# Causal attention in three layers of a decoder: score blocks packed to three quarters, next scores ahead of the other group's transposes

## Chip, cores, metric

One core of one Trainium2 chip runs the whole program. The metric is the device time of one execution in microseconds; the times below are medians. TensorE is written PE (its weight loads PEld), VectorE DVE, ScalarE ACT, GpSimd POOL.

## What is computed

The reference is a decoder of four blocks on x of shape (8, 128, 128): eight sequences of 128 positions with 128 features. Each block is a self-attention-like layer, a cross-attention and a feed-forward layer, all with a layer norm ahead and a residual behind. The change touches the three layers with causal softmax attention, 16 heads of 8 features: the cross-attention of block 0 (L0x, with rotated queries and keys), the self-attention of block 1 (L1a) and of block 3 (L3a, rotated as well). Their core is

```python
scores = jnp.einsum('bhqd,bhkd->bhqk', Q, K) / sqrt(d)
scores = jnp.where(causal, -jnp.inf, scores)      # causal: key behind query
probs = jax.nn.softmax(scores, axis=-1)
heads = jnp.einsum('bhqk,bhkd->bhqd', probs, V)
```

Two other layers (L1x, L2x) run the same loop without a causal mask, and the change leaves theirs as it was.

## The kernel before

The eight sequences are two groups of four (`GB = 4`). Each group has its own tiles and its own four of the eight PSUM banks. Every engine runs one program for each group, and `weave` merges the two by hand-written due times: each piece of a program yields `(layer, time)` and the smallest goes next into that engine's queue. Queues are in order, so these times are the order of the work. Engines wait for each other through named steps (`s.step(name)`, `s.at(name)`).

An attention layer first makes queries and keys with features on partitions (`QT`, `KT`), values with positions on partitions and a column of ones behind each head (`vaug`, written from bank 2 by ACT in `values`, L931), and `KTm`, the keys of one sequence spread over heads (`first_keys`, L1287, on DVE; the later ones on POOL in `spread_keys`, L353). Four heads sit in a strip of 32 rows, so one matmul of a strip, with `KTm` as the moving operand, gives the scores of four heads.

Then comes `attend`: for each sequence b of each group a "turn", numbered `turn = 2*b + g`, 0 to 7 in a layer, the two groups by turns. In one turn:

- PE writes the mask into the four banks (`masked`, L441, bf16, 512 columns each) and adds the scores (`scores`, L450, four f32 matmuls of 512 columns, one for each strip and bank): heads 0 to 15, 128 queries on partitions, 128 keys each.
- DVE takes, half by half (two banks, eight heads), the maximum of each row (L1322) and subtracts it into `pr` (L1326).
- PE turns the eight 128x128 blocks of the half (`turned`, L457, transposes at L461) back into the same banks, so that keys lie on partitions. I call the halves' transposes T0 and T1.
- ACT takes the exponential into `PT` (`exponentials`, L937): one instruction of 1024 elements for the first half (L944), two of 512 for the second (L948).
- PE multiplies with the values (`weighted`, L465, eight matmuls a half into 32-column strips, here PV0 and PV1), ACT reads the result (`weighted_out`, L950, L911), and the turn's banks are free for the mask and scores of the group's next turn.

The order on PE is set in `attend` at L501 to L518: T0 at due time `beat(turn - 1, 5)`, then at `beat(turn, 0)` T1, PV0, a mask, PV1 and two masks, and at `beat(turn, 6)`, which is behind the T0 of the other group (`beat(turn, 5)`), the last mask and the next scores. So the queue reads: T0 of a turn, scores of the other group, T1, PV0, PV1 of that turn, T0 of the next turn, scores, and so on. After turn 6 the results of group 0 are turned back (`back`, L478, 16 transposes) between T0 and T1 of turn 7.

Of the kernel before, what the change touches and what calls it, by code (L numbers as in the profile page):

```python
# [14 lines left out]
P = 128  # L15
B = 8
GB = 4
# [10 lines left out]
MAGIC = 12582912.0  # L28
NEG = -1.0e30
LAYERS = ["pre", "L0a", "L0x", "L0f", "L1a", "L1x", "L1f", "L2a", "L2x", "L2f", "L3a", "L3x", "L3f"]  # L30
DESCENT = 50
# [32 lines left out]
CONSTS = [("ident", P), ("heads", HG), ("heads_x", HG), ("c0", HD), ("s0", HD), ("c3", HD), ("s3", HD), ("keepT", P), ("tri", E0 * E0), ("ident3", E2)]  # L64
BCONSTS = [("identb", P), ("causalb", P), ("alibi", H * P)]

# [26 lines left out]
def build(nc, x_d, ctx_d, mask_d, w_d, r_d, c_d, k_d, b_d, out_d, marks):  # L93
# [35 lines left out]
    class Tiles:  # L129


        def __init__(self, g):
            def own(name, shape, dt=F32):
                return sb(f"{name}{g}", shape, dt)
# [23 lines left out]
            self.vv = own("vv", [P, GB, MH, MD + 1])  # L158
            self.mx, self.rc = own("mx", [P, 2, H // 2]), own("rc", [P, H])
            self.rc3 = own("rc3", [P, GB - 1, H])  # L160
            self.co, self.coT = own("co", [P, GB, P]), own("coT", [P, W4])
# [21 lines left out]
    def pair(g, half):  # L183

        return all_banks[:, 4 * g + 2 * half:4 * g + 2 * half + 2, :]

    def heads_of(pr2):
# [27 lines left out]
    identb = bconst("identb")  # L215
    causalb = bconst("causalb")
    alibi = bconst("alibi").rearrange("p (h k) -> p h k", k=P)
# [53 lines left out]

    def keys_of(t, b):

        return t.KT[:, b * P:(b + 1) * P].unsqueeze(1).to_broadcast([P, HG, P])

    def own_head(l):

        return const("heads_x" if l == "L1x" else "heads").unsqueeze(2).to_broadcast([P, HG, P])

# [34 lines left out]
    def _(pool):  # L314
# [13 lines left out]
        def program(g):  # L328
# [7 lines left out]
            def spread_keys(n, l):  # L336

                first = 0 if l in ("L1x", "L2x") else 1
                for b in range(first, GB):
                    if g == 0 and b == 0 and l in BEHIND:  # L340
                        yield ahead(n, l, 6)
                    else:
                        yield n, ((1 + b if first == 0 else 19) if b < 2 else beat(2 * (b - 2) + g))
                    if b == first:
# [8 lines left out]
                    pool.tensor_tensor(t.KTm[:, b % 2, :, :], keys_of(t, b), own_head(l), ALU.mult).then_inc(*s.step(f"keys{b}"))  # L353
                    if b == 1:
                        yield from add_bias(n, 19, l)
# [43 lines left out]
    def _(pe):  # L399
# [7 lines left out]
        def program(g):  # L407
# [31 lines left out]
            def attend(n, l):  # L439

                def masked(b, r):  # L441

                    out = bank(r)
                    if l == "L1x":
                        mm(out, identb, alibi[:, HG * r:HG * r + HG, :], stop=False)
                    else:
                        mask = t.dmask[:, b, :] if l == "L2x" else causalb
                        mm(out, identb, mask.unsqueeze(1).to_broadcast([P, HG, P]), stop=False)

                def scores(b):  # L450
                    pe.wait_ge(*s.at(f"{l}.keys{b}"))
                    for i in range(GB):
                        r = 32 * i
                        ins = mm(bank(i), QT[r:r + 32, b * P:(b + 1) * P], t.KTm[r:r + 32, b % 2, :, :], start=False, tile_position=(r, 0))
                    ins.then_inc(*s.step(f"S{b}"))

                def turned(u):  # L457
# [41 lines left out]
                masked(0, 0)  # L499
                scores(0)  # L500
                for b in range(GB):  # L501
# [396 lines left out]
    def _(act):  # L898
# [5 lines left out]
        def program(g):  # L904
# [25 lines left out]

            def values():  # L931
                act.wait_ge(*s.at(f"{s.layer}.v"))
                V = bank(2).rearrange("p (b h d) -> p b h d", b=GB, h=H)
                act.activation(t.vaug[:, :, :, 0:HD], V, ACT.Copy).then_inc(*s.step("vaug"))

            def attend(n, l):
# [16 lines left out]

                for b in range(GB):
# [10 lines left out]
            for n, l in enumerate(LAYERS[1:STAGES + 1]):  # L965
# [57 lines left out]
                if l in ("L0x", "L3a"):  # L1023
# [10 lines left out]
                    if l == "L0x" and g == 0:  # L1034
                        read(KT, bank(1), "KTp", "KT")
                    read(QT, bank(0), "QTp", "QT")
                    if l == "L3a" or g == GROUPS - 1:
                        read(KT, bank(1), "KTp", "KT")
                    yield from attend(n, l)
                if l in ("L1a", "L1x", "L2x"):  # L1040
# [6 lines left out]
                    if l == "L1a":  # L1047
                        read(KT, bank(1), "k", "KT")
                        values()
# [107 lines left out]
    def _(dve):  # L1157
# [50 lines left out]
        def program(g):  # L1208
# [78 lines left out]
            def first_keys(l):  # L1287
                dve.wait_ge(*s.at(f"{l}.KT"))
                dve.tensor_tensor(t.KTm[:, 0, :, :], keys_of(t, 0), own_head(l), ALU.mult).then_inc(*s.step("keys0"))

            def attend(n, l):
# [8 lines left out]
                def normal_last():  # L1300
# [5 lines left out]
                                      wide(t.rc[:, :], HD), ALU.mult).then_inc(*s.step(f"co{GB - 1}"))  # L1306

                if l in ("L1a", "L3a"):
                    yield n, 19
                    first_keys(l)  # L1310
                if l in ("L1x", "L2x"):
# [4 lines left out]
                       .then_inc(*s.step("vaug"))  # L1316
                for u in range(UNITS):
                    b, half = divmod(u, 2)
# [399 lines left out]
def constants():  # L1718
# [32 lines left out]
    putb("identb", np.eye(P))  # L1751
    putb("causalb", np.where(r[None, :] > r[:, None], f(NEG), f(0.0)))
    rel = np.abs(r[None, :] - r[:, None]).astype(f)
# [85 lines left out]
```

## Time and profile before

| | us |
|---|---|
| time before, median of 3 runs (655.9 to 656.96) | 656.77 |
| the profiled execution | 654.79 |
| its span, first to last instruction | 653.0 |
| first maximum of turn 0 to the turn-back behind turn 7, layer L1a (176.93 to 220.68) | 43.75 |

The page of the profile gives for each engine the time it was busy, and the chain of work that ended last. The views by stretch and the timelines give start and length of single instructions in microseconds from the start of the span. One layer's loop of eight turns is shown by L1a; L0x (from 81.57) and L3a (from 539.77) repeat it.

### The profile page before, as it was taken

How to read it: one execution, taken by the hardware profiler on the slowest of the kernel's cores; microseconds unless marked ns; L12 is line 12 of the kernel's file. 1: busy time of each engine (PE TensorE's matmuls, PEld its weight loads, DVE VectorE, ACT ScalarE, POOL GpSimd, SP SyncE). 2: the span in 40 equal slices, each digit the busy share in tenths (PEclk: the TensorE clock that was granted, in tenths of full speed). 3: DMA queues.
4: the chain of work that ended last, by engine and by line, in shares of the span. 5: the costliest groups of instructions: out<-in, count | busy, mean ns of one | idle time of the engine just before them, and what ended most of it. 6: DMA issues, size and time to landing. Idle time of an engine off the chain costs nothing.

```text
span 653.0 us, 10939 instructions
## 1 busy us (share of the span) xinstructions
PE 553.2 (85%) x4377; PEld 364.7 (56%) x4377; DVE 467.3 (72%) x1200; ACT 262.8 (40%) x462; POOL 98.3 (15%) x101
## 2 busy tenths in 40 slices
PE   1326789978999999988997899999899978998787
PEld 0324356767455755655786765556345654675435
DVE  7688899777499779964348646996744489976685
ACT  1265645415255435525423353552321024543170
POOL 5012120004410151010002015101100022002210
PEclk9967999999799999999999999999999999999889
DMA  9900000000000000000000000000000000000001
GB/s 271 384 0 2 0 2 1 2 1 1 1 2 2 2 2 1 2 1 1 2 1 1 1 1 1 2 1 1 2 1 1 0 2 1 2 1 1 1 1 32
DMA packets 6721, 11.89 MB, mean 18 GB/s; under 512 B 528, under 2 KB 4880, under 8 KB 6416
## 3 DMA queue, kind: packets, MB, share of 16 engines
q1 hardware_dynamic: 6672, 11.21, 4.9%
q8 instruction: 34, 0.56, 0.4%
q14 instruction: 15, 0.12, 0.1%
HBM read 10.68 MB, written 0.52 MB: 17 GB/s over the span
## 4 chain that ended last, share of the span: by engine, by line
PE 62%; DVE 26%; ACT 5%; POOL 3%; issue 2%; DMA 1%; SPq 1%; DVEq 0%; ACTq 0%
PE ps L401 45%; PE ps L461 10%; DVE st L1215 3%; DVE big L1326 3%; PE ps L417 3%; DVE mx L1322 3%; PE ps L481 2%; DVE xn L1412 2%; POOL rs L334 2%; DVE x L1339 1%; DMA co<-in_ctx 1%; DVE mv L1218 1%; PE ps L608 1%; DVE ve L1220 1%; DVE s L1558 1%
## 5 line engine op out<-in xcount | busy, mean ns | idle before, releaser
L1322 DVE TENSOR_REDUCE mx<-ps 128x8 f32<-128x1024 f32 x80 | 97.4, 1218 | 13.5 <-PE ps L401 13.5
L1326 DVE TENSOR_TENSOR big<-ps,mx 128x1024 f32<-128x1024 f32 x80 | 98.0, 1225 | 6.9
L401 PE MATMUL ps<-bt 128*128 128x512 bf16 x304 | 88.2, 388 | 9.2 <-DVE ve L1220 3.9
L461 PEld LDWEIGHTS ps<-kt,big 128*128 128x128 f32 x640 | 71.1, 141 | 43.6 <-DVE big L1326 36.3
L461 PE MATMUL ps<-kt,big 128*128 128x128 f32 x640 | 85.5, 276 | 8.3 <-DVE big L1326 8.3
L334 POOL TENSOR_TENSOR rs<-ve,negh 128x4 f32<-128x4 f32 x26 | 26.4, 1015 | 371.4 <-DVE ve L1220 371.3
L401 PE MATMUL ps<-xnT,wt 128*128 128x512 f32 (+1 forms) x140 | 67.0, 606 | 5.1 <-DVE big L1604 2.6
L944 ACT ACTIVATE big<-ps 128x1024 f32<-128x1024 f32 x40 | 40.9, 1024 | 56.2 <-PE ps L461 56.2
L401 PEld LDWEIGHTS ps<-wt,big 128*128 128x128 f32 (+1 forms) x480 | 56.0, 191 | 8.5 <-issue 7.9
L401 PE MATMUL ps<-wt,big 128*128 128x128 f32 (+1 forms) x480 | 60.3, 279 | 0.0
L948 ACT ACTIVATE big<-ps 128x512 f32<-128x512 f32 x80 | 43.4, 595 | 34.5 <-PE ps L461 34.5
L353 POOL TENSOR_TENSOR KTm<-qk,kt 128x512 f32<-128x512 f32 x34 | 37.4, 1110 | 95.5 <-PE ps L401 55.8
L401 PE MATMUL ps<-big,vaug 128*32 128x128 f32 x1280 | 51.6, 279 | 0.1
L401 PEld LDWEIGHTS ps<-bt 128*128 128x128 bf16 x304 | 26.5, 99 | 42.9 <-issue 16.7
L401 PE MATMUL ps<-KTm,qk 32*128 32x512 f32 x320 | 45.6, 640 | 0.0
L911 ACT ACTIVATE xnT<-ps 128x512 f32<-128x512 f32 (+1 forms) x40 | 19.6, 490 | 61.8 <-PE ps L417 59.1
L1385 DVE SCALAR_TENSOR_TENSOR x<-ps,gw,x 128x128 f32<-128x128 f32 x80 | 22.2, 343 | 29.8 <-PE ps L401 29.0
L401 PEld LDWEIGHTS ps<-xnT,wt 128*128 128x128 f32 (+1 forms) x140 | 24.1, 189 | 29.5 <-issue 19.2
L1339 DVE TENSOR_TENSOR x<-ps,x 128x512 f32<-128x512 f32 x16 | 11.1, 691 | 39.9 <-PE ps L401 39.9
L401 PEld LDWEIGHTS ps<-big,vaug 128*32 128x32 f32 x1280 | 30.0, 109 | 16.3 <-ACT big L948 9.5
L1412 DVE TENSOR_SCALAR xn<-x,mv,rs 128x128 f32<-128x128 f32 x96 | 28.1, 356 | 9.0 <-POOL rs L334 8.3
L401 PE MATMUL ps<-wt,xnT 128*128 128x128 f32 (+2 forms) x256 | 31.2, 275 | 3.1 <-DVE big L1560 1.5
(276 smaller groups left out, 775.3 us busy)
## 6 DMA issues: line engine op xcount, KB each, us to landing
wt<-in_weights SPq DMA_DIRECT2D x1, 1664.0 KB, 15.2
wt<-in_weights SPq DMA_DIRECT2D x1, 1603.0 KB, 9.9
wt<-in_weights SPq DMA_DIRECT2D x6, 256.0 KB, 9.1
rowt<-in_rows SPq DMA_DIRECT2D x1, 975.0 KB, 5.7
wt<-in_weights SPq DMA_DIRECT2D x1, 832.0 KB, 11.5
wt<-in_weights SPq DMA_DIRECT2D x1, 608.0 KB, 16.3
wt<-in_weights SPq DMA_DIRECT2D x1, 580.0 KB, 5.5
x<-in_x SPq DMA_DIRECT2D x2, 256.0 KB, 3.1
```

What stands on the lines that cost most here:

```text
L334: pool.tensor_tensor(out, src, negh[:, :], ALU.pow).then_inc(*s.step(name + "_r"))
L353: pool.tensor_tensor(t.KTm[:, b % 2, :, :], keys_of(t, b), own_head(l), ALU.mult).then_inc(*s.step(f"keys{b}"))
L401: return pe.matmul(out, lhsT, rhs, start=start, stop=stop, **k)
L417: ins = pe.transpose(seq(bk, b), src[:, b, :], ident)
L461: ins = pe.transpose(heads_of(pair(g, u % 2))[:, i, j, :], pr[:, (u % 2) * HH + HG * i + j, :], ident)
L911: act.activation(out, src, ACT.Copy).then_inc(*s.step(name))
L944: act.activation(P2, T2, ACT.Exp, scale=SCALES[l][half]).then_inc(*s.step(f"exp{u}.1"))
L948: act.activation(P2[:, i, :, :], T2[:, i, :, :], ACT.Exp, scale=SCALES[l][half]).then_inc(*s.step(f"exp{u}.{i}"))
L1322: dve.tensor_reduce(top, S, AX.X, ALU.max).then_inc(*s.step())
L1326: dve.tensor_tensor(pr[:, half * HH:(half + 1) * HH, :].rearrange("p (i j) k -> p i j k", i=2), S, top.unsqueeze(3).to_broadcast([P, 2, HG ...
L1385: dve.scalar_tensor_tensor(x[:, b, :], bank(banks[e])[:, b * P:(b + 1) * P], gw[:, b, e:e + 1], x[:, b, :], ALU.mult, ALU.add).then_inc(*s ...
L1412: dve.tensor_scalar(xn[:, b, :], x[:, b, :], t.mv[:, b, 0:1], t.rs[:, b:b + 1], ALU.subtract, ALU.mult).then_inc(*s.step("xn"))
```

## The change

For the layers in `CAUSAL` queries 0 to 63 ("early") no longer meet keys 64 to 127, which the mask made zero anyway. Scores of four heads then fill 384 columns of a bank instead of 512, on two half strips of partitions: partitions 0 to 63 hold the first two heads of a strip, 64 to 127 the other two; each has two blocks of 128 keys for late queries and two of 64 for early ones.

- Scores become 16 f32 matmuls on tiles of 32 rows and 64 columns, eight of 256 columns and eight of 128; the mask covers 256 columns of a bank.
- The maximum is taken for a whole turn at once: 1024 elements for late and 512 for early queries; each half is subtracted in two instructions (256 and 512 elements).
- Three transposes a bank instead of four.
- Exponentials: one of 512 elements and two of 256 (on 64 partitions each) for the first half, two of 256 and two of 256 on 64 partitions for the second. The products wait for the whole half.
- For odd heads the two halves of the keys lie exchanged. So ACT writes the keys twice (`KTw`, 512 and 256 columns), and the values of even heads alone; DVE writes those of odd heads with the halves exchanged (`odd_values`, two copies of 256 elements on 64 partitions, due ahead of `first_keys` in L1a and L3a).
- POOL zeroes a part of `PT` in L0x and L3a (`blank`).
- The next scores are due at `beat(turn, 4)`, ahead of the other group's T0 at `beat(turn, 5)`.

The core of the diff:

```diff
+                def packed_scores(b):
+                    pe.wait_ge(*s.at(f"{l}.keys{b}"))
+                    for late in (1, 0):
+                        for pairs_of in range(2):
+                            for i in range(GB):
+                                r = 32 * i
...
+                                ins = mm(out, Q, K, start=False, tile_position=(r, HK * pairs_of), skip_group_check=True)
+                    ins.then_inc(*s.step(f"S{b}"))
...
+                for b in range(GB if l in CAUSAL else 0):
+                    turn, more = 2 * b + g, b + 1 < GB
+                    yield n, beat(turn - 1, 5)
+                    packed_turned(2 * b)
+                    yield n, beat(turn, 0)
+                    packed_turned(2 * b + 1)
+                    packed_weighted(2 * b)
+                    if more:
+                        masked(b + 1, 1)
+                    packed_weighted(2 * b + 1)
+                    if more:
+                        masked(b + 1, 3)
+                        pe.wait_ge(*s.at(f"{l}.OT{2 * b}"))
+                        masked(b + 1, 0)
+                        yield n, beat(turn, 4)
+                        pe.wait_ge(*s.at(f"{l}.OT{2 * b + 1}"))
+                        masked(b + 1, 2)
+                        packed_scores(b + 1)
...
+            def keys(need):
+                read(t.KTw[:, :, 0:P], four(bank(1)), need, "KTn")
+                read(t.KTw[:, :, P:P + HK], four(bank(1))[:, :, 0:HK], need, "KT")
...
+                    if half == 0:
+                        act.wait_ge(*s.at(f"{l}.T{u}.1"))
+                        act.activation(P2[:, :, :, HK:P], T2[:, :, 0:4, :], ACT.Exp, scale=scale).then_inc(*s.step())
+                    else:
+                        for i in range(2):
+                            act.wait_ge(*s.at(f"{l}.T{u}.{i}"))
+                            act.activation(P2[:, i, :, HK:P], T2[:, i, 0:4, :], ACT.Exp, scale=scale).then_inc(*s.step())
...
+                    for c in range(2):
+                        rows = slice(c * HK, (c + 1) * HK)
+                        act.activation(P2[rows, :, 2 * c:2 * c + 2, 0:HK], T2[rows, :, 4:6, :], ACT.Exp, scale=scale).then_inc(*s.step(f"exp{u}"))
...
+            def odd_values(l):
+                dve.wait_ge(*s.at(f"{l}.v"))
+                dve.wait_ge(*s.at(f"{l}.vaug_even"))
...
+                dve.tensor_copy(t.vaug[early, :, 1:H:2, 0:HD], V[late, :, 1:H:2, :]).then_inc(*s.step())
+                dve.tensor_copy(t.vaug[late, :, 1:H:2, 0:HD], V[early, :, 1:H:2, :]).then_inc(*s.step("vaug"))
...
+                        dve.tensor_reduce(of_late, late, AX.X, ALU.max).then_inc(*s.step())
+                        dve.tensor_reduce(of_early, early, AX.X, ALU.max).then_inc(*s.step())
```

## Rows read from the trace of the kernel before

**Rows 1.** The page: engines (busy us, share, instructions); shares of the chain

```profile
PE 553.2 (85%) x4377; PEld 364.7 (56%) x4377; DVE 467.3 (72%) x1200; ACT 262.8 (40%) x462; POOL 98.3 (15%) x101
...
PE 62%; DVE 26%; ACT 5%; POOL 3%; issue 2%; DMA 1%; SPq 1%; DVEq 0%; ACTq 0%
```

**Rows 2.** Busy time of one turn of L1a: us, engines (instructions), clock, DMA

```profile
187.05:192.25 5.20, 5.20 (x64) 3.13 (x60) 4.80 (x4) 2.83 (x5) 1.04 (x1) 1.00 0.00 0
```

**Rows 3.** Timeline of PE over that turn: start us, length us, instruction, count

```profile
187.05 1.09 PE L461 MATMUL ps<-kt,big 128*128 128x128 f32 x8
188.07 0.64 PE L401 MATMUL ps<-big,vaug 128*32 128x128 f32 x16
188.65 0.39 PE L401 MATMUL ps<-bt 128*128 128x512 bf16 x1
188.97 0.64 PE L401 MATMUL ps<-big,vaug 128*32 128x128 f32 x16
189.54 0.61 PE L401 MATMUL ps<-bt 128*128 128x512 bf16 x2
189.99 1.04 PE L461 MATMUL ps<-kt,big 128*128 128x128 f32 x8
190.86 0.38 PE L401 MATMUL ps<-bt 128*128 128x512 bf16 x1
191.17 1.14 PE L401 MATMUL ps<-KTm,qk 32*128 32x512 f32 x8
192.25 0.33 PE L461 MATMUL ps<-kt,big 128*128 128x128 f32 x1
```

**Rows 4.** Timeline of ACT over the same turn

```profile
187.74 1.08 ACT L948 ACTIVATE big<-ps 128x512 f32<-128x512 f32 x2 [0.85 <-PE ps L461]
...
189.68 0.38 ACT L911 ACTIVATE td<-ps 128x256 f32<-128x256 f32 x1 [0.51 <-PE ps L401]
191.12 1.02 ACT L944 ACTIVATE big<-ps 128x1024 f32<-128x1024 f32 x1 [1.06 <-PE ps L461]
```

**Rows 5.** Timeline of DVE over the same turn

```profile
188.51 1.23 DVE L1326 TENSOR_TENSOR big<-ps,mx 128x1024 f32<-128x1024 f32 x1
189.66 1.21 DVE L1322 TENSOR_REDUCE mx<-ps 128x8 f32<-128x1024 f32 x1
```

**Rows 6.** Groups by line and shape: busy us, mean ns, idle before

```profile
L1282 DVE TENSOR_TENSOR big<-ps,kt 128x256 f32<-128x256 f32 x8 | 3.0, 414 | 0.0
L1654 DVE TENSOR_REDUCE s<-ps 128x4 f32<-128x512 f32 x2 | 1.4, 686 | 2.9 <-PE ps L401 2.9
...
L1145 ACT ACTIVATE big<-ps,colt 64x512 f32<-64x512 f32 x2 | 1.4, 682 | 0.3 <-PE ps L401 0.3
```

**Rows 7.** Timeline of L1a: T0 of turns 1 and 6, end of the loop

```profile
184.80 1.04 PE L461 MATMUL ps<-kt,big 128*128 128x128 f32 x8
...
210.82 1.04 PE L461 MATMUL ps<-kt,big 128*128 128x128 f32 x8
...
220.68 0.66 PE L417 MATMUL ps<-kt,co 128*128 128x128 f32 x4
```

**Rows 8.** Timeline ahead of the first turn of L1a

```profile
174.97 0.60 ACT L934 ACTIVATE vaug<-ps 128x512 f32<-128x512 f32 x1 [0.29 <-PE ps L401]
...
175.72 1.14 PE L401 MATMUL ps<-KTm,qk 32*128 32x512 f32 x8
...
176.93 1.22 DVE L1322 TENSOR_REDUCE mx<-ps 128x8 f32<-128x1024 f32 x1 [1.53 <-PE ps L401]
```

**Rows 9.** Timeline of DVE ahead of the first turn, L0x, then L3a

```profile
78.83 0.69 DVE L1289 TENSOR_TENSOR KTm<-qk,kt 128x512 f32<-128x512 f32 x1
...
80.23 0.69 DVE L1289 TENSOR_TENSOR KTm<-qk,kt 128x512 f32<-128x512 f32 x1 [0.71 <-ACT qk L911]
...
81.57 1.23 DVE L1322 TENSOR_REDUCE mx<-ps 128x8 f32<-128x1024 f32 x1 [0.64 <-PE ps L401]
...
539.77 1.22 DVE L1322 TENSOR_REDUCE mx<-ps 128x8 f32<-128x1024 f32 x1 [0.64 <-PE ps L401]
```

More of the change, by code:

```diff
@@ L29 @@
 NEG = -1.0e30
+CAUSAL = ("L0x", "L1a", "L3a")
+HK = P // 2
+PK = 6 * HK
 LAYERS = ["pre", "L0a", "L0x", "L0f", "L1a", "L1x", "L1f", "L2a", "L2x", "L2f", "L3a", "L3x", "L3f"]
@@ L215, in build @@
     identb = bconst("identb")
[L216 removed]
+    corner = bconst("corner")
     alibi = bconst("alibi").rearrange("p (h k) -> p h k", k=P)
@@ L343, in spread_keys @@
                         yield n, ((1 + b if first == 0 else 19) if b < 2 else beat(2 * (b - 2) + g))
+                    if b == first and l in ("L0x", "L3a"):
+                        pool.wait_ge(*s.at(f"{l}.qrot"))
+                        pool.wait_ge(*s.at(f"{l}.krot"))
+                        pool.memset(t.PT[:, :, 0:HK], 0.0).then_inc(*s.step("blank"))
                     if b == first:
@@ L499, in attend @@
                 masked(0, 0)
-                scores(0)
-                for b in range(GB):
+                if l in CAUSAL:
+                    packed_scores(0)
+                else:
+                    scores(0)
+                for b in range(GB if l in CAUSAL else 0):
[16 more added lines that the diff above has]
+                        packed_scores(b + 1)
+                for b in range(0 if l in CAUSAL else GB):
                     turn, more = 2 * b + g, b + 1 < GB
@@ L952, in weighted_out, with packed_exponentials @@
                     read(t.ot[b][:, 2 * half * P:2 * (half + 1) * P], bank(2 * half)[:, 0:2 * P], f"O{u}", f"OT{u}")
-                for b in range(GB):
+                def packed_exponentials(u):
+                    half = u % 2
+                    P2 = PT[:, half * HH:(half + 1) * HH, :].rearrange("p (i j) k -> p i j k", i=2)
+                    T2 = packed(pair(g, half))
+                    scale = SCALES[l][half]
+                    if u >= 2:
+                        act.wait_ge(*s.at(f"{l}.O{u - 2}"))
+                    if half == 0:
+                        act.wait_ge(*s.at(f"{l}.T{u}.1"))
+                        act.activation(P2[:, :, :, HK:P], T2[:, :, 0:4, :], ACT.Exp, scale=scale).then_inc(*s.step())
+                    else:
+                        for i in range(2):
+                            act.wait_ge(*s.at(f"{l}.T{u}.{i}"))
+                            act.activation(P2[:, i, :, HK:P], T2[:, i, 0:4, :], ACT.Exp, scale=scale).then_inc(*s.step())
+                    if u < 2 and l in ("L0x", "L3a"):
+                        act.wait_ge(*s.at(f"{l}.blank"))
+                    for c in range(2):
+                        rows = slice(c * HK, (c + 1) * HK)
+                        act.activation(P2[rows, :, 2 * c:2 * c + 2, 0:HK], T2[rows, :, 4:6, :], ACT.Exp, scale=scale).then_inc(*s.step(f"exp{u}"))
+                for b in range(GB if l in CAUSAL else 0):
+                    turn = 2 * b + g
+                    yield n, beat(turn - 1, 5)
+                    packed_exponentials(2 * b)
+                    yield n, beat(turn, 0)
+                    packed_exponentials(2 * b + 1)
+                    weighted_out(2 * b)
+                    weighted_out(2 * b + 1)
+                for b in range(0 if l in CAUSAL else GB):
                     turn = 2 * b + g
@@ L1047, in program @@
                     if l == "L1a":
-                        read(KT, bank(1), "k", "KT")
+                        keys("k")
                         values()
@@ L1316, in attend @@
                        .then_inc(*s.step("vaug"))
-                for u in range(UNITS):
+                for u in range(UNITS if l in CAUSAL else 0):
+                    b, half = divmod(u, 2)
+                    yield n, beat(2 * b + g, 1 + half)
+                    blocks, strips = all_banks[:, GB * g:GB * (g + 1), 0:PK], slice(2 * half, 2 * half + 2)
+                    late = bass.AP(tensor=blocks.tensor, offset=blocks.offset, ap=[blocks.ap[0], blocks.ap[1], [4 * HK, 2], [1, P]])
+                    early = blocks[:, :, 2 * HK:4 * HK].rearrange("p i (c k) -> p i c k", c=2)
+                    of_late, of_early = (t.mx[:, k, :].rearrange("p (i c) -> p i c", i=GB) for k in range(2))
+                    if half == 0:
+                        dve.wait_ge(*s.at(f"{l}.S{b}"))
+                        dve.tensor_reduce(of_late, late, AX.X, ALU.max).then_inc(*s.step())
+                        dve.tensor_reduce(of_early, early, AX.X, ALU.max).then_inc(*s.step())
+                        dve.wait_ge(*s.last())
+                    if u >= 2:
+                        dve.wait_ge(*s.at(f"{l}.T{u - 2}.1"))
+                    out = pr.rearrange("p (i j) k -> p i j k", i=GB)[:, strips, :, :]
+                    dve.tensor_tensor(out[:, :, 1, :].rearrange("p i (c k) -> p i c k", c=2), early[:, strips, :, :],
+                                      of_early[:, strips, :].unsqueeze(3).to_broadcast([P, 2, 2, HK]), ALU.subtract).then_inc(*s.step())
+                    dve.tensor_tensor(out[:, :, 0:3:2, :], late[:, strips, :, :],
+                                      of_late[:, strips, :].unsqueeze(3).to_broadcast([P, 2, 2, P]), ALU.subtract).then_inc(*s.step(f"sub{u}"))
+                for u in range(0 if l in CAUSAL else UNITS):
                     b, half = divmod(u, 2)
```

61 lines of the change are left out of this document (51 added, 10 removed).

## Prediction

> **What bounds the kernel now.** Start with the page: PE is busy 85% of the span, DVE 72%, and the chain that ended last runs 62% over PE and 26% over DVE [rows 1]. An average hides the stages, so next take one turn in the middle of L1a: 5.20 us, PE busy 5.20 of them, DVE 4.80, ACT 2.83, clock 1.00 [rows 2]. Then the timeline of PE in that turn shows what the 5.20 are: T1 from 187.05, PV0 from 188.07, a mask, PV1, two masks, the other group's T0 from 189.99, a mask, the scores from 191.17, and the next T1 at 192.25 [rows 3]. No step waits: each starts when the one ahead has left the array. ACT works beside it: the long exponential (191.12 to 192.14) lies under the scores, the short pair under T1 and PV0 [rows 3, 4]. So PE's own work sets the turn, DVE has 0.4 us to spare, and ACT's time, 2.83, costs nothing as long as PE has something else to do meanwhile.
>
> **The work of a turn after the change.** PE: eight transposes follow each other at 0.109 us (189.99 to 190.86) [rows 3]; four fewer of sixteen save 0.44. Masks: two in a row take 0.45, so one of 512 columns 0.22, and half the columns save 0.11 each, 0.43 for four. PV0 and PV1 stay at 0.57 each. Scores take 1.08 now, in two passes of 512 columns at 0.43 each (a pass over 128 columns takes 0.109) and some 0.2 to load and drain [rows 3]. Afterwards each of eight tiles takes two passes of 256 and two of 128 columns, 0.65 in all; if all eight run at once the scores take 0.75 to 0.87, and I take 0.80. No row shows eight tiles at once: the nearest are four strips of columns (the products, 16 records in 0.57) and four of rows (the scores themselves). If tiles in the same rows took turns it would be 1.45. With 0.80 PE's own work falls from 5.20 to about 4.05 us a turn.
>
> DVE: 1024 elements take 1.22, a step 1.15 behind the one ahead (188.51 to 189.66) [rows 5]; 512 take 0.69 and 256 take 0.41 [rows 6]. A turn is then maxima 1.14 + 0.69 + 0.10 and twice 0.33 + 0.61 for the subtractions, 3.9 us. T0 can start 3.01 after the first maximum starts instead of 2.54, T1 0.94 behind it.
>
> ACT: 512 elements 0.60, two of them 1.08, so 0.49 apart; 256 take 0.38 [rows 4], and with the same overlap of 0.10 are 0.28 apart. An instruction on 64 partitions is no shorter: 64x512 takes 0.68 [rows 6]. The seven exponentials of a turn take 0.49 + 5 x 0.28 + 0.38 = 2.27 in a row.
>
> **Where the new order puts them.** Now the due times. Behind PV1 and the masks stand, at `beat(turn, 4)`, the wait for the last read of the results, the last mask and the next scores; only then, at `beat(turn, 5)`, T0 of the other group. Queued behind that wait are all of PE's next pieces. What PE ran beside the exponentials, the other group's scores between T0 and T1, is now ahead of T0. From T0 on nothing but T1 (0.65) and PV0 is left to cover 2.27 us of exponentials. The cover is gone, so the loop goes through ACT and back:
>
> - T0 start to first exponential: six transposes 0.65, 0.06 for the load behind the scores, and 0.26 from the end of the slot to ACT (190.86 to 191.12) [rows 3, 4]: 0.97
> - seven exponentials: 2.27; handover to PV1: 0.06 (bounds 0.05 and 0.15, the pair ending at 188.82 ahead of PV1 at 188.97 [rows 3, 4])
> - PV1 to ACT's read: 0.71 (188.97 to 189.68); the read 0.38; handover 0.06 [rows 3, 4]
> - last mask 0.21, scores 0.80, and the next T0 starts.
>
> Sum 0.97 + 2.27 + 0.06 + 0.71 + 0.38 + 0.06 + 0.21 + 0.80 = 5.46 us a turn against 5.20: PE waits about 1.4 us in each. DVE's 3.01 from the scores to T0 lies beside this and is covered; if it were not, this path alone would be scores 0.80 + 3.01, below 5.46.
>
> **One layer.** Before, L1a takes 7.87 us from the first maximum (176.93) to T0 of turn 1 (184.80), 26.02 to T0 of turn 6 (210.82), 9.86 to the end of its loop (220.68) [rows 7, 8]. After: the start is 3.01 + 0.97 + 2.27 + 0.06 to PV1, then 0.71 + 0.38 + 0.06 + 0.21 + 0.80, together 8.47, so +0.60. Five turns 5 x 5.46 = 27.30, so +1.28. The end has no further scores: 3.30 to PV1 of turn 6, 0.57, T0 of turn 7 0.65, 16 turn-backs 1.75, half of T1 and the handover 0.59, four exponentials 1.26, PV1 0.7: 8.8, so -1.06, since DVE held T0 and T1 there before. A layer's loop: +0.82; three layers: +2.5 us.
>
> **Ahead of the loop.** In L1a the values left ACT at 174.97 + 0.60, off the path; the scores started at 175.72 and DVE at 176.93 [rows 8]. Now the even heads' copy ends at 175.35, then DVE's two copies 0.74, then the keys' product 0.69 (0.08 overlapped), the scores 0.80, and handovers of 0.06: the first maximum at 177.68, +0.75. The wait for these copies stands in PE's queue ahead of masks and scores, and in DVE's ahead of the keys' product. In L0x DVE sits idle 0.71 and 0.64 between its key products and the first maximum [rows 9]; four copies of 0.33 to 0.41 and a key read that ends 0.28 later leave the first maximum at 81.91 instead of 81.57: +0.34, and the same in L3a, whose idle times are alike [rows 9]. Bounds for the three: 0.3 (all in idle time) and 2.5 (each like L1a's). POOL's zeroing and its key products have over a turn's time; I put them at nothing, and at 0.5 us if they slow DVE. ACT's second key read is in the 0.28. Sum ahead of the loops: +1.4.
>
> Total: 654.79 + 2.5 + 1.4 = 658.7 on the profiled execution, whose span is 653.0 with 1.8 us around it. It lies 2.0 below the median of the runs shown, so I add the 3.9 to 656.77: **660.7 us**.
>
> **Rivals.** First, the waits are covered after all: PE starts the other group's transposes while the last mask waits. Then a turn costs PE's own 4.05 us, and a layer 0.6 - 5 x 1.15 - 1.06 = -6.2; with +1.4 ahead the time is 639.6. For it: PE and DVE do lose a fifth of their work. Against it: every group of matmuls starts in the order of the queue, none ahead of one that stands before it [rows 3]. Chance 0.13, with all values over 0.2% faster.
>
> Second, tiles that share rows take turns, so that packing doesn't pay on PE: scores of 1.45 instead of 0.80. Six scores of a layer lie on the loop, 18 x 0.65 = +11.7: 672.4. A value between (pairs of passes overlap, 1.03) gives 664.8. Chance 0.20 for both. The products speak against it: 16 records on all 128 rows take 0.57, where 16 single passes of 0.109 would take 1.74 [rows 3], so tiles in the same rows, but other columns, do run together. The Trainium skill ("TensorE: Matmul & The Clock Gate", Part 3, The mechanism) says that weight loads overlap with running matmuls only where the row group differs. By that rule the second case holds; the products' rows disagree with it, and that is why it has no more than 0.15 of these 0.20.
>
> Third, no difference: exponentials 0.26 apart and scores 0.75 take 0.05 + 0.12 off each turn; over 18 turns that is -3.1, and copies hidden in idle time take another 1: 656.6. Chance 0.10.
>
> The forecast, ACT in the loop with all eight tiles at once, has 0.57: 658.2 to 664, the upper end with handovers of 0.15 (18 x 0.18). Within 0.2% (1.3 us) is about what a measurement can't tell from no change. So slower 0.57 + 0.20 = 0.77, within 0.10, faster 0.13. The range 656.0 to 672.5 takes in the bounds of scores and handovers and leaves out the first rival and little above.
>
> **What would show it.** In the profile after: a turn of 5.4 to 5.6 us in which PE is busy no more than 4.3 with a wait for ACT ahead of PV0, PV1 and the last mask, and the chain running over ACT in the three layers; DVE near 3.9; scores of 0.8 us, 1.45 in the second rival. A turn near 4.1 with PE full would mean the first rival. A lower clock than 1.00 in the loop, since PE idles more, or a DVE that ends last, would make me wrong in a way that no sum here has.

## The result, and the profile after

| | before | after |
|---|---|---|
| median of four executions | 656.87 us | 673.16 us |
| profiled execution | 654.79 us, span 653.0 | 673.12 us, span 671.3 |
| granted clock, mean over the span | 0.972 | 0.957 |
| PE busy | 553.2 us | 540.1 us |
| DVE busy | 467.3 us | 448.4 us |
| ACT busy | 262.8 us | 275.7 us |

The changed kernel is slower: ratio 1.0236, interval 1.0201 to 1.0271, where 660.7 (1.006) was forecast. One of the four executions took 1042.06 us and is left out of this ratio; the other three average 672.2 us, and nothing below explains the slow one.

PE and DVE have less to do, as intended, and the median went up by 16.3 us. The page of the changed kernel (engines, then shares of the chain; its answer before is [rows 1]) shows the shift from PE to ACT:

```profile
PE 540.1 (80%) x4850; PEld 367.2 (55%) x4857; DVE 448.4 (67%) x1260; ACT 275.7 (41%) x564; POOL 100.7 (15%) x105
...
PE 51%; DVE 25%; ACT 15%; issue 4%; POOL 3%; DMA 1%; SPq 1%; DVEq 0%; ACTq 0%
```

ACT's share of the chain rose from 5% to 15%, PE's fell from 62% to 51%. One undisturbed turn of L1a, timeline of PE and ACT together (start, length, instruction, count, idle time before and what ended it), to be read against [rows 3, 4]:

```profile
218.50 1.53 PE L505 MATMUL ps<-kt,big 128*128 128x128 f32 x12
...
219.47 0.60 ACT L1053 ACTIVATE big<-ps 128x512 f32<-128x512 f32 x1 [2.08 <-PE ps L505]
...
219.96 0.77 ACT L1062 ACTIVATE big<-ps 64x256 f32<-64x256 f32 x2
...
220.76 0.66 ACT L1057 ACTIVATE big<-ps 128x256 f32<-128x256 f32 x2
...
220.78 0.65 PE L425 MATMUL ps<-big,vaug 128*32 128x128 f32 x16 [0.76 <-ACT big L1062]
...
221.30 0.77 ACT L1062 ACTIVATE big<-ps 64x256 f32<-64x256 f32 x2
...
222.13 0.64 PE L425 MATMUL ps<-big,vaug 128*32 128x128 f32 x16 [0.48 <-ACT big L1062]
...
222.84 0.38 ACT L996 ACTIVATE xn<-ps 128x256 f32<-128x256 f32 x1 [0.35 <-PE ps L425]
...
223.28 0.28 PE L425 MATMUL ps<-bt 128*128 128x256 bf16 x1 [0.18 <-ACT xn L996]
...
223.49 0.91 PE L425 MATMUL ps<-KTm,qk 32*64 32x256 f32 x32
```

PE waits for ACT three times in the turn: 0.76 ahead of PV0, 0.48 ahead of PV1, 0.18 ahead of the last mask. The next T0 starts at 224.33, so the turn takes 5.83 us. Five turns of L1a from the busy-time view (stretch, length, busy us of PE, PEld, DVE, ACT, POOL, then granted clock, DMA share, GB/s), the answer to [rows 2]:

```profile
193.79:199.56 5.77, 4.41 (x89) 2.94 (x81) 3.77 (x6) 3.30 (x9) 1.04 (x1) 1.00 0.00 0
199.56:206.18 6.62, 5.20 (x89) 3.23 (x81) 3.77 (x6) 3.30 (x9) 1.04 (x1) 0.86 0.01 2
206.18:212.67 6.49, 5.17 (x88) 3.70 (x81) 3.77 (x6) 3.30 (x9) 0.00 (x0) 0.88 0.00 0
212.67:218.50 5.83, 4.41 (x89) 2.94 (x81) 3.77 (x6) 3.30 (x9) 0.00 (x0) 1.00 0.01 3
218.50:224.33 5.83, 4.41 (x89) 2.94 (x81) 3.77 (x6) 3.30 (x9) 0.00 (x0) 1.00 0.01 3
```

PE is busy 4.41 of 5.83 where it was busy 5.20 of 5.20. Two of the turns are longer by 0.79 and 0.66 because the clock was at its lower level (1.2 GHz) in part of them.

The loops run from the first maximum of a layer to the turn of its outputs. Their marks in the changed kernel, first DVE (the maxima of L1a and L3a), then PE; before they are in [rows 7 to 9]:

```profile
185.09 1.23 DVE L1455 TENSOR_REDUCE mx<-ps 128x8 f32<-128x1024 f32 x1 [0.47 <-PE ps L425]
...
555.72 1.22 DVE L1455 TENSOR_REDUCE mx<-ps 128x8 f32<-128x1024 f32 x1 [1.14 <-PE ps L425]
```

```profile
233.52 0.65 PE L441 MATMUL ps<-kt,co 128*128 128x128 f32 x4
...
603.36 0.66 PE L441 MATMUL ps<-kt,co 128*128 128x128 f32 x4
```

With the same marks in all layers the 18.3 us between the two spans divide as follows:

| stretch | before | after | more |
|---|---|---|---|
| start to L0x's first maximum | 81.57 | 82.03 | 0.46 |
| L0x's loop | 43.72 | 49.10 | 5.38 |
| to L1a's first maximum | 51.64 | 53.96 | 2.32 |
| L1a's loop | 43.75 | 48.43 | 4.68 |
| to L3a's first maximum | 319.09 | 322.20 | 3.11 |
| L3a's loop | 43.72 | 47.64 | 3.92 |
| rest | 69.5 | 68.0 | -1.5 |

14.0 of the 18.3 us lie in the three loops, for which 2.5 were forecast. The stretches ahead of L1a and L3a hold the starts of these layers. L1a's start, from PE's last projection of the inputs to the first maximum, takes 4.24 us (180.85 to 185.09) where it took 3.05 (173.88 to 176.93), so +1.19 at a clock of 1.00. L3a's start, from PE's last rotation of queries and keys, takes 4.98 (550.74 to 555.72) where it took 2.65 (537.12 to 539.77), so +2.33. Ahead of L1a's start the clock was at its lower level for some 10 us against some 7 before (0.57 over 153 to 161 us and 0.66 over 170 to 175 us; before, 0.51 over 163 to 170); the other 1.13 us of that stretch lie there.

### The profile page after: what moved, and what is told of

Read it like the earlier page. It is cut to its first block, busy times and chain, and to the rows that moved or that the text cites. A ratio compares the mean times of both kernels' runs of the same rounds, so it can differ in the third digit from the quotient of the medians.

```text
span 671.3 us, 12049 instructions
## 1 busy us (share of the span) xinstructions
PE 540.1 (80%) x4850; PEld 367.2 (55%) x4857; DVE 448.4 (67%) x1260; ACT 275.7 (41%) x564; POOL 100.7 (15%) x105
## 4 chain that ended last, share of the span: by engine, by line
PE 51%; DVE 25%; ACT 15%; issue 4%; POOL 3%; DMA 1%; SPq 1%; DVEq 0%; ACTq 0%
PE ps L425 38%; ACT big L1062 4%; PE ps L525 4%; PE ps L505 4%; DVE st L1333 3%; PE ps L441 2%; ACT big L1057 2%; DVE xn L1560 2%; POOL rs L354 2%; PE ps L545 2%; DVE x L1487 1%; ACT big L1053 1%; DVE big L1474 1%; DVE mx L1470 1%; DMA co<-in_ctx 1%
## 5 line engine op out<-in xcount | busy, mean ns | idle before, releaser
L425 PE MATMUL ps<-bt 128*128 128x512 bf16 (+1 forms) x297 | 76.5, 356 | 12.7 <-DVE ve L1338 3.1
L1455 DVE TENSOR_REDUCE mx<-ps 128x8 f32<-128x1024 f32 x24 | 29.4, 1223 | 40.1 <-PE ps L425 40.1
L425 PE MATMUL ps<-KTm,qk 32*64 32x256 f32 (+2 forms) x896 | 42.7, 406 | 3.6 <-DVE KTm L1407 3.6
L505 PE MATMUL ps<-kt,big 128*128 128x128 f32 x288 | 41.5, 297 | 3.8 <-DVE big L1463 3.8
L1470 DVE TENSOR_REDUCE mx<-ps 128x8 f32<-128x1024 f32 x32 | 39.0, 1219 | 6.1 <-PE ps L425 6.0
L1474 DVE TENSOR_TENSOR big<-ps,mx 128x1024 f32<-128x1024 f32 x32 | 39.2, 1224 | 3.1 <-DVE mx L1470 0.5
L505 PEld LDWEIGHTS ps<-kt,big 128*128 128x128 f32 x288 | 34.9, 153 | 8.9 <-DVE big L1463 5.5
L1053 ACT ACTIVATE big<-ps 128x512 f32<-128x512 f32 x24 | 14.4, 598 | 60.9 <-PE ps L505 60.9
L525 PEld LDWEIGHTS ps<-kt,big 128*128 128x128 f32 x256 | 28.4, 141 | 16.0 <-DVE big L1474 12.3
L425 PE MATMUL ps<-wt,xnT 128*128 128x128 f32 (+2 forms) x256 | 34.0, 291 | 3.1 <-DVE big L1708 1.5
L425 PEld LDWEIGHTS ps<-wt,xnT 128*128 128x128 f32 x256 | 32.6, 207 | 6.9 <-ACT xnT L996 3.2
```

Source lines behind the costliest of these rows:

```text
L425: return pe.matmul(out, lhsT, rhs, start=start, stop=stop, **k)
L505: ins = pe.transpose(out[:, (0, 2, 1)[k] * P:((0, 2, 1)[k] + 1) * P], pr[:, 4 * (2 * half + i) + k, :], ident)
L525: ins = pe.transpose(heads_of(pair(g, u % 2))[:, i, j, :], pr[:, (u % 2) * HH + HG * i + j, :], ident)
L1053: act.activation(P2[:, :, :, HK:P], T2[:, :, 0:4, :], ACT.Exp, scale=scale).then_inc(*s.step())
L1455: dve.tensor_reduce(of_late, late, AX.X, ALU.max).then_inc(*s.step())
L1470: dve.tensor_reduce(top, S, AX.X, ALU.max).then_inc(*s.step())
```

## The experiments

Turn and loops of all kernels, from their traces (a turn at clock 1.00, loops as they came, slower turns included):

| kernel | turn | L0x | L1a | L3a | median | ratio to before |
|---|---|---|---|---|---|---|
| before | 5.20 | 43.72 | 43.75 | 43.72 | 656.87 | |
| after | 5.83 | 49.10 | 48.43 | 47.64 | 673.16 | 1.0236 |
| e1, order undone | 4.86 | 41.83 | 41.41 | 41.41 | 650.98 | 0.9913 |
| e2, order alone | 5.70 | 46.31 | 46.31 | 46.31 | 663.96 | 1.0097 |
| e3, waits filled | 5.83 | 47.37 | 47.37 | 48.67 | 671.34 | 1.0204 |
| e4, exponentials on all partitions | 5.48 | 45.03 | 44.43 | 44.43 | 660.84 | 1.0080 |
| e5, e1 and values on ACT | 4.86 | 41.85 | 41.39 | 41.38 | 642.56 | 0.9818 |
| e6, e5 and PE filled at the start | 4.86 | 41.39 | 41.40 | 41.40 | 647.33 | 0.9868 |
| e7, e1 with one maximum | 4.51 | 38.55 | 38.55 | 38.70 | 641.26 (one) | |
| e8, values on ACT, order as changed | 5.83 | 47.41 | 46.97 | 47.62 | 667.71 | 1.0182 |
| e9, the code of e5 again | 4.86 | 41.78 | 41.40 | 41.40 | 643.89 | 0.9834 |

### The order undone (e1_order_back)

```
-                        yield n, beat(turn, 4)
+                        yield n, beat(turn, 6)
```

> The changed kernel with one line undone: the next scores are due at beat(turn, 6) again, behind the other group's first transposes; everything packed stays. If the loss comes from the order (ACT's exponentials of 2.66 us a turn have no cover and PE waits 1.4 us for them), the other group's mask and scores, 0.21 + 0.84, lie beside them again: from T0 0.91 to the first exponential, 2.66 to PV1, then 0.57 and 0.21 to the next T0, so 4.3 to 4.5 us a turn where the changed kernel has 5.8 and the kernel before 5.20, PE busy nearly throughout, clock 1.00 in the three loops, and a time of 641 to 650 us, below the kernel before. If instead the packed pieces are dearer than they look (scores in eight tiles, seven exponentials, exchanged values), the turn stays at 5.2 or above and the time at 657 to 673.

650.98 us, ratio 0.9913 (0.9882 to 0.9944). One line turns a loss of 2.4% into a gain of 0.9%, so the order is what makes the packing lose, and packing itself gains. The turn came down to 4.86, not to 4.3 to 4.5, and the time lies 1 us above the expected span. The busy-time view of one turn, then rows of the timeline of PE and its weight loads (PEld):

```profile
196.80:201.66 4.86, 4.38 (x83) 2.89 (x81) 3.77 (x7) 3.31 (x10) 0.00 (x0) 1.00 0.01 3
```

```profile
199.58 0.64 PEld L505 LDWEIGHTS ps<-kt,big 128*128 128x128 f32 x6 [0.41 <-DVE big L1463]
199.58 0.88 PE L505 MATMUL ps<-kt,big 128*128 128x128 f32 x6
...
200.50 0.91 PE L425 MATMUL ps<-KTm,qk 32*64 32x256 f32 x32
```

The weight loads of T0 now wait 0.41 for DVE's subtraction. From T0 to the scores 0.92, from the scores to the next maximum 1.01, from there to the next T0 2.93: 4.86. A path through DVE has taken ACT's place; e7 tests that.

### The order alone (e2_order_alone)

```
-                        yield n, beat(turn, 6)
+                        yield n, beat(turn, 4 if l in ("L0x", "L1a", "L3a") else 6)
```

> The kernel before with the order alone: next scores due at beat(turn, 4) in the three causal layers, nothing packed. If the order costs by itself: T0 to the first exponential 1.13 (eight transposes 0.87, 0.26 to ACT), the long exponential 0.92, the two short ones 0.49 + 0.60, PV1 to the read 0.71, read and handover 0.44, two masks 0.3, scores 1.08, together 5.6 to 5.8 us a turn against 5.20: 18 turns make +8 to +10, 664 to 667 us, up to 671 if the clock falls in the loops as in the changed kernel. If the order is harmless and the packing is what costs: 655 to 658.

663.96 us, ratio 1.0097 (1.0066 to 1.0127), the turn 5.70 as expected; the time is just below the expected 664 to 667. The same wait, without anything packed, in PE's timeline:

```profile
199.99 1.14 PE L401 MATMUL ps<-KTm,qk 32*128 32x512 f32 x8
201.06 1.97 PE L461 MATMUL ps<-kt,big 128*128 128x128 f32 x16
203.32 0.64 PE L401 MATMUL ps<-big,vaug 128*32 128x128 f32 x16 [0.30 <-ACT big L944]
...
205.69 0.71 PE L401 MATMUL ps<-KTm,qk 32*128 32x512 f32 x4
```

T0 and T1 follow each other, PV0 waits for ACT, and the next scores come only at 205.69, 5.70 behind those of 199.99. The order costs 2.6 us a layer by itself.

### The exponentials of 64 partitions (e4_full_rows)

```
-                        rows = slice(c * HK, (c + 1) * HK)
+                        rows = slice(0, P)
```

> The changed kernel with the four exponentials of 64 partitions a turn made on all 128 partitions, the same number, columns and order. They then also write the blocks that must stay zero, so the weights of keys 64 to 127 for queries 0 to 63 and the sums are not the reference's. If the 0.33 us a turn beyond the forecast comes from instructions on 64 partitions that do not overlap with their neighbours (0.39 to 0.41 apart where 128 partitions are 0.26 to 0.28 apart), the turn falls from 5.8 to 5.4 to 5.5 and the time to 665 to 668. If it comes from the form of the operand (two pieces of 64 elements), the spacing stays at 0.39 and the time within 0.3% of 673.

660.84 us, ratio 1.0080 (1.0048 to 1.0113): lower than the expected 665 to 668. The turn is 5.48, as expected, and 0.02 off the 5.46 of the prediction. (This kernel also writes the blocks of `PT` that must stay zero, so it computes something else.) ACT's timeline:

```profile
201.50 0.60 ACT L1053 ACTIVATE big<-ps 128x512 f32<-128x512 f32 x1 [2.08 <-PE ps L505]
202.00 0.66 ACT L1062 ACTIVATE big<-ps 128x256 f32<-128x256 f32 x2
202.52 0.68 ACT L1057 ACTIVATE big<-ps 128x256 f32<-128x256 f32 x2
203.05 0.71 ACT L1062 ACTIVATE big<-ps 128x256 f32<-128x256 f32 x2
```

On 128 partitions the pair at 202.00 gives way to the next after 0.52; on 64, with the same columns, after 0.80 (219.96 to 220.76). Twice as many elements take less time in a row, since here each instruction starts before the one ahead has ended. From the first exponential to PV1 it is 2.31 us (201.50 to 203.81) against 2.66. Between loops without a change of clock, e8's 46.97 and e4's 44.43 in L1a, this is 2.54 us a layer, 7.6 in three. The three loops together are 11.3 us shorter; what goes beyond 7.6 is the slower turns, which this trace does not have in the middle of a loop.

### PE's waits filled (e3_filled)

```
+                            ins = idle(7, out)       # behind T1
+                    idle(4, bank(1))                 # ahead of PV1
+                        idle(3, bank(1))             # ahead of the wait for the read
+                        ins = idle(20, bank(1))      # behind the first scores
```

These are the added lines, with remarks; each `idle` gives that many products of 128 columns. Those in `bank(1)` write into the bank that collects mask and scores of one strip, and the output isn't the reference's.

> The changed kernel with work added on PE alone: small products of 128 columns into a part of a bank that nobody reads, seven behind T1, four ahead of PV1, three ahead of the wait for the read, in every turn of the causal layers, and twenty behind the first scores. They fill waits and compute nothing that is used. If PE's waits in the loops make the granted clock fall (0.50 for some 3.5 us in L0x and L1a and 5 us at L3a's and L0x's starts, worth 4.2 us in the three loops), the clock stays near 1.00 in the loops and the time falls to 666 to 670, although PE has more to do. If the clock falls for another reason, the stretches at 0.50 stay and the time is 673 or, where a filler ends late, up to 680.

671.34 us, ratio 1.0204 (1.0164 to 1.0244): the time fell by less than expected (666 to 670). Busy time of a turn:

```profile
204.06:209.89 5.83, 5.19 (x102) 3.82 (x94) 3.77 (x6) 3.30 (x9) 0.00 (x0) 1.00 0.01 3
```

PE is busy 5.19 of 5.83, the turn is no longer for it, and the two slow turns are gone from L0x and L1a: 47.37 in both, 1.7 and 1.1 less; L3a's loop, with a clock below 1.00 at its start, is 1.0 longer. That alone would speak for the waits as the cause. But e8, below, has the waits and no filler, and its turns in the middle of these loops are at 1.00 as well. So this run doesn't show that the waits of a turn make the clock fall.

### The values exchanged on ACT (e5_act_values, e8_values_alone, e9_act_values_again)

In e5 and e9, which are the same code, the order is undone as in e1; in e8 it is left as changed. The lines that move:

```
-                dve.tensor_copy(t.vaug[early, :, 1:H:2, 0:HD], V[late, :, 1:H:2, :])...
-                dve.tensor_copy(t.vaug[late, :, 1:H:2, 0:HD], V[early, :, 1:H:2, :])...
+                act.activation(t.vaug[early, :, 1:H:2, 0:HD], V[late, :, 1:H:2, :], ACT.Copy)...
+                act.activation(t.vaug[late, :, 1:H:2, 0:HD], V[early, :, 1:H:2, :], ACT.Copy)...
```

In the changed kernel four copies stand on DVE's queue ahead of the two keys' products of L3a. DVE's timeline, then POOL's:

```profile
550.72 0.43 DVE L1414 COPY vaug<-ps 64x256 f32<-64x256 f32 x1
551.18 0.42 DVE L1415 COPY vaug<-ps 64x256 f32<-64x256 f32 x1
551.63 0.43 DVE L1414 COPY vaug<-ps 64x256 f32<-64x256 f32 x1
552.09 0.42 DVE L1415 COPY vaug<-ps 64x256 f32<-64x256 f32 x1
552.53 2.04 DVE L1407 TENSOR_TENSOR KTm<-KTw,kt 128x512 f32<-128x512 f32 x2
```

```profile
552.39 1.04 POOL L377 TENSOR_TENSOR KTm<-KTw,kt 128x512 f32<-128x512 f32 x1 [0.63 <-ACT KTw L996]
```

> The order undone as in e1_order_back, and the exchange of the odd heads' values moved from DVE to ACT (two copies of 64 partitions behind ACT's copy of the even heads). In the changed kernel the four copies stand on DVE from 550.72 to 552.53 ahead of L3a's keys products, while ACT is idle 0.86 and 1.51 us there. If they are what moves L3a's first maximum by +2.33 (with the clock, which falls to 0.50 in the wait), L3a's scores start 1.5 to 2 us earlier relative to its last turn of keys, L0x's 0.3 earlier, L1a's about the same: 647.5 to 649.5 us against 651.0 of e1_order_back, the turns unchanged at 4.86. If the copies lie beside other waits, or delay ACT's reads of the keys as much, 651 within 1 us.

642.56 us, ratio 0.9818 (0.9773 to 0.9863), 5 us below the expected 647.5 to 649.5. The same place in DVE's timeline:

```profile
530.67 0.69 DVE L1410 TENSOR_TENSOR KTm<-KTw,kt 128x512 f32<-128x512 f32 x1
532.29 0.69 DVE L1410 TENSOR_TENSOR KTm<-KTw,kt 128x512 f32<-128x512 f32 x1 [0.93 <-ACT KTw L996]
532.90 1.21 DVE L1447 TENSOR_REDUCE mx<-ps 128x8 f32<-128x1024 f32 x1
```

The products stand right behind the rotation, the second waits 0.93 for ACT's read, and from the end of L2x's loop to the first maximum of L3a it is 94.05 us against 96.27 in e1 and 94.30 in the kernel before. So the exchange on DVE was most of the +2.33. A part of it is the clock: in the changed kernel the first scores and their handover take 1.69 at the lower level (554.03 to 555.72), in e5 1.18 at 1.00 (531.72 to 532.90). ACT does the exchange in idle time.

L1a lost to the exchange as well, at a clock of 1.00. The two keys' products stand behind both groups' copies, and the scores behind them; rows of the timeline of all engines, the changed kernel, then e5:

```profile
180.85 1.05 PE L425 MATMUL ps<-wt,xnT 128*128 128x128 f32 x8
...
182.43 0.43 DVE L1414 COPY vaug<-ps 64x256 f32<-64x256 f32 x1 [1.74 <-ACT vaug L1020]
182.88 0.42 DVE L1415 COPY vaug<-ps 64x256 f32<-64x256 f32 x1
183.33 1.29 DVE L1407 TENSOR_TENSOR KTm<-KTw,kt 128x512 f32<-128x512 f32 x2
...
184.08 0.91 PE L425 MATMUL ps<-KTm,qk 32*64 32x256 f32 x32 [1.74 <-DVE KTm L1407]
```

```profile
169.92 1.05 PE L425 MATMUL ps<-wt,xnT 128*128 128x128 f32 x8
...
171.34 0.91 PE L425 MATMUL ps<-KTm,qk 32*64 32x256 f32 x32
...
172.35 1.23 DVE L1447 TENSOR_REDUCE mx<-ps 128x8 f32<-128x1024 f32 x1 [0.64 <-PE ps L425]
```

L1a's start is 4.24 us with the exchange on DVE and 2.43 with it on ACT (169.92 to 172.35), against 3.05 before. L0x's, from the last rotation, is 3.20 and 2.18 against 2.63. Of the 7.8 us between the traces of e1 and e5, 4.9 lie in the three starts (1.0, 1.8 and 2.0, the last with a change of clock); the other 3.0 lie ahead of them, in stretches that the edit leaves alone (24 to 36 us, for one, at 0.51 in e1 and 1.00 in e5).

> The changed kernel with the exchange of the odd heads' values on ACT instead of DVE, the order left as it is (scores ahead of the other group's transposes). If the exchange on DVE is a term of its own, L3a's first maximum comes 2.0 to 2.5 us earlier relative to the end of L2x's loop, as it did between e1_order_back and e5_act_values (96.27 to 94.05), L0x's and L1a's 0 to 0.4 earlier, the turns stay at 5.8, and the time falls from 673.2 to 668 to 671. If the gain of e5_act_values came from elsewhere, 673 within 1.5 us.

667.71 us, ratio 1.0182 (1.0151 to 1.0213), just below the span expected. From the end of L2x's loop L3a's first maximum comes 1.7 us earlier than in the changed kernel (95.30 against 96.98), with the clock at its lower level ahead of it in both (0.57 over 543 to 547 us here). That is less than the expected 2.0 to 2.5; L0x's and L1a's starts fall by 1.0 and 1.8, more than the expected 0 to 0.4. The turns stay at 5.83. One turn of L1a:

```profile
200.74:206.57 5.83, 4.41 (x83) 2.94 (x82) 3.77 (x7) 3.30 (x9) 0.00 (x0) 1.00 0.01 3
```

PE waits here just as long as in the changed kernel's turns, and the clock is 1.00 throughout.

> The same code as e5_act_values, timed in five rounds. Its trace was 7.8 us shorter than that of e1_order_back, and only 2.6 of them lie between the end of a layer and the first maximum of L0x and L3a; the rest is time at a granted clock of 0.50 in stretches that the edit does not touch (24 to 36 us and 144 to 152 us of e1_order_back). If those stretches come and go between executions, the median here lies between 642 and 648 us; if they belong to the code, 642 to 643.

643.89 us, ratio 0.9834 (0.9808 to 0.9860), executions from 642.64 to 647.84. So the time of the same code varies by some 5 us. That stretches at the lower clock come and go with it isn't shown: both traces of this code (e5, e9) are 640.8 us long, and the mean clocks of the other executions don't follow their times (0.987 at 647.27 us, 0.965 at 643.67).

### PE filled at the start of a loop (e6_values_fill)

On top of e5:

```
+                    if b == 0 and g == GROUPS - 1:
+                        for _ in range(20):
+                            ins = mm(bank(1)[:, PK:4 * P], identb, identb, start=False, ...)
```

> As e5_act_values, and twenty small products on PE behind the second group's first scores of each causal layer, into columns that nobody reads, where PE otherwise waits for the first subtraction. If the stretches at 0.50 at the start of L0x's loop (84.9 to 88.6 in the changed kernel) come from that wait, they go there, the loop of L0x falls from 41.83 to the 41.41 of L1a, and the time is 0.4 to 1.5 us below e5_act_values. If the clock falls for what lies ahead of the loop, nothing changes within 0.5 us.

647.33 us, ratio 0.9868 (0.9852 to 0.9885): slower than e5, not faster, yet in L0x the step did what it was to do. The same four microseconds of L0x, e5, then e6, and the fill in e6's timeline of PE:

```profile
85.00:89.00 4.00, 4.00 (x43) 2.70 (x44) 3.52 (x6) 3.08 (x9) 0.00 (x0) 0.57 0.00 0
```

```profile
85.00:89.00 4.00, 3.03 (x47) 1.96 (x46) 3.96 (x7) 3.03 (x9) 0.13 (x1) 1.00 0.00 0
```

```profile
82.72 1.29 PE L425 MATMUL ps<-bt 128*128 128x128 bf16 x20
84.61 1.80 PE L508 MATMUL ps<-kt,big 128*128 128x128 f32 x12 [0.60 <-DVE big L1458]
```

Without the fill PE waits 1.83 us ahead of T0 and the clock is at 0.57 of full speed just behind it; with it the wait is 0.60 and the clock stays at 1.00, and L0x's loop takes 41.39 instead of 41.85. The other traces agree: with waits of 1.57 to 1.83 ahead of this first T0 (the changed kernel, e1, e4, e5, e8, e9) the clock fell there each time, with 0.35 to 0.97 (before, e2, e3, e6, e7) it did not. So at the start of L0x the lower clock depends on this wait. But the same wait (1.65 or 1.66) stands ahead of the first T0 of L1a in these six traces, and there the clock stayed at 1.00, so a wait of this length alone doesn't bring it down; what else differs isn't shown. The trace of e6 is 4.3 us longer than that of e5, and the longer stretches lie where the code is the same (24 to 36, 164 to 168, 532 to 536 and 600 to 606 us in part at the lower level in e6; e5 has that only ahead of L1a, 0.69 over 161 to 165). They are not explained.

### One maximum instead of two (e7_one_maximum)

```
-                        dve.tensor_reduce(of_early, early, AX.X, ALU.max)...
-                                      of_early[:, strips, :]...
+                                      of_late[:, strips, :]...
```

> As e1_order_back, without the second maximum of a turn (queries 0 to 63 subtract the maxima of the other half, so the output is not the reference's). In e1_order_back a turn takes 4.86 us, PE waits 0.41 us ahead of each T0 for DVE's subtraction, and from the scores to T0 DVE takes 1.01 + 2.93. If that path sets the turn (scores, two maxima, the subtractions, T0, the next scores), leaving out 0.69 to 0.8 of it brings PE's own 4.4 forward: a turn of 4.3 to 4.5 us, three loops of some 38.5, and 641 to 645 us. If ACT's exponentials set it, the turn stays at 4.8 to 4.9 and the time at 649 to 652.

641.26 us in one execution, loops of 38.55 to 38.70; the turn is at the upper end of what was expected. One turn:

```profile
200.72:205.23 4.51, 4.16 (x81) 2.94 (x81) 3.17 (x6) 3.30 (x10) 0.00 (x0) 1.00 0.01 4
```

DVE is busy 0.60 less and the turn falls by 0.35, from 4.86 to 4.51: the path through DVE did set e1's turn. What is left of PE's waits in these turns is one of 0.35 ahead of PV1, for ACT, so the next path, through ACT, lies 0.35 us below that through DVE. (Queries 0 to 63 use the wrong maxima here, and the output isn't the reference's.)

## Why the prediction was right, and why it was too small

**The size.** The direction and the path were right, the size was not: +3.9 us was forecast, and the median rose by 16.3. The three executions of the ratio average 672.2, just inside the range, which ends at 672.5; their median, 673.1, lies just outside. That end of the range comes from the second rival, which did not happen, so that the range reaches this far is luck. Of the signs that were named, the waits for ACT at the three places, the scores of 0.8 and DVE near 3.9 came; the turn (5.83 for 5.4 to 5.6), PE's busy time (4.41 for no more than 4.3) and the clock did not.

**The path.** The forecast named a loop through ACT, and the trace shows it term by term (forecast, then the turn from 218.50): T0 to the first exponential 0.97, measured 0.97; exponentials and handover 2.33, measured 2.66; PV1 to the read 0.71, measured 0.71; read and handover 0.44, measured 0.44; last mask 0.21, measured 0.21; scores 0.80, measured 0.84. The sum is 5.83 instead of 5.46. DVE's 3.77 (forecast 3.9) and PE's 4.41 (forecast 4.05) were not what set it. e1 and e2, which move the one due time in either direction, show that the order makes the path.

**The term that was mis-sized.** It is the exponentials: "256 take 0.38 [rows 4], and with the same overlap of 0.10 are 0.28 apart", applied to those of 64 partitions, too. Those are 0.39 to 0.41 apart. The row cited for them (64x512 takes 0.68, [rows 6]) gave a length, and it was read as if the overlap with the next came along with it. Four such instructions in a turn cost 0.35 us, 7.6 us in three layers, and e4, in which only the partitions differ, takes it away: with it the loop of L1a is 0.68 above that of before, where the sum had 0.82.

**Ahead of the loops.** L0x +0.46 for +0.34, L1a +1.19 for +0.75, L3a +2.33 for +0.34. In L1a the path was the forecast one, its pieces were longer: DVE's two copies take 0.90 to the keys' product (182.43 to 183.33) instead of 0.74, and from the scores to the maximum it is 1.01 instead of 0.86. In L3a the step "and the same in L3a, whose idle times are alike" failed. DVE's idle time of 0.64 to 0.65 was there, but in L3a DVE comes to the copies of both groups at once, straight from the rotation, so 1.8 us of copies stood ahead of both keys' products and could not use it. Behind them DVE's first product ran beside one of POOL's and the pair took 0.75 us longer than in L1a, a term put at nothing, or at 0.5. e5 removes the copies.

**The clock.** The prediction said that a clock below 1.00 in the loops would be outside its sums. It was: 1.45 us in the middle of L0x and as much in L1a, 0.67 at the start of L0x and as much of L3a, 4.2 together. The stretches outside the loops and their starts add 0.4 net: 1.1 ahead of L1a's start and 1.5 back at the end, where the time at the lower level is some 3 us longer and shorter than before, and 0.8 between L1a's loop and L3a's start, where the clock was 1.00 in both kernels (0.4 of it in L1x's loop, 44.11 for 43.72, and not explained). Two of the stretches in the loops from the changed kernel's busy-time view, L0x and L3a:

```profile
85.00:89.00 4.00, 3.84 (x29) 3.02 (x29) 3.96 (x8) 2.39 (x7) 0.00 (x0) 0.59 0.00 0
553.00:562.00 9.00, 7.35 (x92) 5.04 (x96) 7.79 (x12) 2.33 (x6) 2.51 (x3) 0.50 0.00 0
```

At the start of L0x filling PE's wait keeps the clock up (e6). For the turns in the middle the cause is open: the waits were there in e8, too, and the clock held. It is open for L3a's start as well, where the clock fell in e6 and e8, too, and not in e5 and e9.

Together: 3.9 forecast, 7.6 for the exponentials, 4.2 for the clock in the loops, 2.5 more at the three starts (0.1, 0.4 and 2.0), 0.4 outside, and 0.3 less in the rest of the loops come to the 18.3 us between the spans.

**The rivals.** The first, PE finding other work meanwhile, did not come: the queue kept its order. The second gave nearly the measured time (672.4) for the wrong reason. Tiles that share rows do not take turns: 32 passes of scores take 0.84 us to the next T0 (223.49 to 224.33), not 1.45. The Trainium skill's rule of "TensorE: Matmul & The Clock Gate", Part 3, The mechanism, by which weights load beside running products only where the row group differs, is not borne out by these scores. The Trainium skill ("TensorE: Matmul & The Clock Gate", Why this matters for your kernels) also says that row and column tiles combine; the trace agrees, with 0.84 us for the eight tiles. The third, no difference, is excluded by the interval.

## What to carry to other kernels

Before counting what an edit saves on the bounding engine, ask what that engine ran while it would otherwise have waited, and whether the new order still has it there: here the packing gained 6 us under the old order and lost 16 under the new one. A duration from a row is the price of an instruction on a path only if the row shows the distance to the next one, in the same shape and on the same partitions. Copies that only move data belong on the engine that is idle there: on ACT the exchange takes nothing from the starts, on DVE it cost 1.0 to 2.0 us in each. The version to keep is e5, with the old order and the exchange on ACT: 0.9834 of the kernel before over six executions (e9, interval 0.9808 to 0.9860).

## What the hardware showed that was not expected

- An exponential of 256 columns on 64 partitions starts 0.39 to 0.41 us ahead of the next instruction, on 128 partitions 0.26 to 0.28; the lengths are 0.36 to 0.38 and 0.38 to 0.45. The Trainium skill ("ScalarE: Activation LUTs", What ACT_TABLE_LOAD costs) gives an overlap of about 93 ns for instructions in a row; the exponentials on 128 partitions agree with 0.10 or more, those on 64 do not overlap.
- DVE's keys' product takes 0.69 us alone (530.67) and the pair at 552.53, beside POOL's product of the same shape, 2.04 instead of the 1.29 that a pair takes at 183.33 in L1a. There POOL's had started first (552.39). Where DVE's starts first, POOL's is the longer one: in the kernel before DVE takes 0.69 from 172.10, and POOL's product from 172.14 takes 1.54 instead of the 1.04 it takes at 176.98.
- The same code took from 641.91 to 647.84 us in ten executions (e5, e9), and in stretches that no edit touches the granted clock differs between traces (24 to 36 us: 0.51 in e1 and e6, 1.00 in e5). A difference of medians below 5 us needs the marks of a trace beside it.
